# A key-maximum pass over pairs of context chunks: relu of a score difference on ScalarE, add and maximum on VectorE, four PSUM bank pairs in turn, and context loads issued from GpSimd's queue

## What is computed

```python
q = (query @ Wq + bq).reshape(B, Nq, H, D)            # H = 16 heads, D = 16
k = (key_value @ Wk + bk).reshape(B, Nkv, H, D)       # Nkv = 12544
attn = clip(einsum('bhqd,bhkd->bhqk', q, k) * scale, -10000, 10000)
attn = softmax(attn, axis=-1)
x = einsum('bhqk,bhkd->bqhd', attn, v).reshape(B, Nq, Cq) @ Wo + bo
```

## Time and profile before

| | before |
|---|---|
| median of three runs | 1149.45 us |
| the profiled execution's own time | 1144.78 us |
| its span, first to last instruction | 1142.9 us |
| TensorE matmul busy over the span | 944.5 us (83%) |
| VectorE busy | 645.1 us (56%) |
| ScalarE busy | 537.1 us (47%) |
| GpSimd busy | 173.4 us (15%) |
| mean granted TensorE clock | 0.927 |

### The profile page before, as it was taken

One profiled execution on the slowest core, in us unless ns is written; L12 is line 12 of the kernel. 1 busy time (PEld: TensorE's weight loads), 2 busy tenths in 40 slices (PEclk: granted clock), 3 DMA queues, 4 the chain that ended last, 5 costly groups with the idle time before them and its releaser, 6 DMA issues.

```text
span 1142.9 us, 21211 instructions
## 1 busy us (share of the span) xinstructions
PE 944.5 (83%) x7651; PEld 699.5 (61%) x7651; DVE 645.1 (56%) x936; ACT 537.1 (47%) x626; POOL 173.4 (15%) x93
## 2 busy tenths in 40 slices
PE   3878888758999999999988758885999989999414
PEld 2545555536777777777756546554887868887303
DVE  5778999872111122222252144994878767778592
ACT  2787888627666666666645512100333323333011
POOL 4000000131111111111175022133003030000000
PEclk9988999779999999999998769998999999999765
DMA  7213121154565665555634332112001000000000
GB/s 211 74 42 122 48 71 57 32 129 87 130 140 130 144 145 128 128 128 128 143 82 98 112 102 56 29 50 55 1 1 38 1 6 1 1 1 1 1 0 5
DMA packets 37319, 81.73 MB, mean 72 GB/s; under 512 B 9553, under 2 KB 17426, under 8 KB 37138
## 3 DMA queue, kind: packets, MB, share of 16 engines
q1 hardware_dynamic: 37266, 81.01, 28.5%
HBM read 41.54 MB, written 0.13 MB: 36 GB/s over the span
## 4 chain that ended last, share of the span: by engine, by line
PE 44%; issue 20%; DVE 11%; SPq 9%; ACT 8%; DMA 6%; POOL 1%; DVEq 1%; ACTq 0%; POOLq 0%
PE ps L1498 9%; SPq L310 8%; DMA ks<-khl 6%; PE ps L1291 5%; PE ps L1508 5%; PE ps L1519 4%; PE ps L1303 4%; PE ps L1245 4%; PE ps L1273 4%; PE ps L1500 2%; DVE cm L813 1%; ACT pr L555 1%; ACT oacc L555 1%; PE ps L1282 1%; ACT khl L592 1%
## 5 line engine op out<-in xcount | busy, mean ns | idle before, releaser
L617 ACT ACTIVATE pr<-ps 128x1024 f32<-128x1024 f32 x196 | 199.9, 1026 | 131.6 <-DVEq L966 128.2
L1291 PE MATMUL ps<-qs,ks 128*128 128x256 f32 x784 | 146.4, 309 | 23.2 <-DMA ks<-khl 14.6
L1245 PE MATMUL ps<-ks 128*128 128x448 f32 x448 | 135.2, 424 | 32.3 <-ACT pr L555 13.5
L1291 PEld LDWEIGHTS ps<-qs,ks 128*128 128x128 f32 x784 | 106.0, 190 | 66.3 <-issue 38.1
L1498 PE MATMUL ps<-ks,ct 128*128 128x512 f32 x448 | 126.1, 404 | 6.9 <-issue 4.2
L813 DVE TENSOR_REDUCE cm<-ps 128x1 f32<-128x896 f32 x112 | 120.7, 1085 | 16.1 <-PE ps L1245 14.7
L1245 PEld LDWEIGHTS ps<-ks 128*128 128x128 f32 x448 | 80.8, 206 | 75.4 <-DVE cm L813 25.1
L1303 PE MATMUL ps<-pr,v 128*17 128x128 f32 x3136 | 125.3, 278 | 0.2 <-ACT pr L617 0.2
L847 DVE SCALAR_TENSOR_TENSOR khl<-ps,bk,khl 128x448 fp32r<-128x448 f32 x56 | 38.2, 683 | 151.5 <-ACT khl L592 151.5
L695 ACT ACTIVATE pr<-ps 128x1024 f32<-128x1024 f32 x56 | 57.6, 1029 | 110.5 <-DVE ps L1096 109.7
L405 POOL TENSOR_TENSOR ct<-raw,ct 128x896 fp32r<-128x896 f32 x14 | 30.6, 2188 | 498.5 <-ACT ct L537 498.5
(11 more groups left out here) (260 smaller groups left out, 1307.4 us busy)
## 6 DMA issues: line engine op xcount, KB each, us to landing
ks<-khl SPq DMA_DIRECT2D x168, 224.0 KB, 4.8
raw<-in_ctxT SPq DMA_DIRECT2D x36, 448.0 KB, 3.8
raw<-in_ctxT SPq DMA_DIRECT2D x54, 224.0 KB, 4.3
ffw<-in_mask_q SPq DMA_DIRECT2D x1, 1568.0 KB, 9.3
ffw<-in_W1T SPq DMA_DIRECT2D x1, 1024.0 KB, 4.9
ffw<-in_W2T SPq DMA_DIRECT2D x1, 1024.0 KB, 7.3
pr<-in_Wq SPq DMA_DIRECT2D x1, 1024.0 KB, 5.0
pr<-in_Wkt SPq DMA_DIRECT2D x1, 1024.0 KB, 7.3
```

What stands on the lines that cost most here:

```text
L617: nc.scalar.activation(pr[:, (HALVES * b + u) % 4, :], bank(2 * (u % 2), 2), ACT.Exp).then_inc(S["e0_exp"], 1)
L1245: last = mm(ps[:, bank + n, 0:NB], qn[:, h, :], kn[:, b, t, n * NB:(n + 1) * NB], start=True, stop=True)
L1291: last = mm(ps[:, 2 * z + k // 2, (k % 2) * 256:(k % 2) * 256 + 256], ks_v[:, b, gg, t * P:(t + 1) * P], qs[:, gg * 256:gg * 256 + 256], s ...
```

## The change

- The pass goes over seven pairs of chunks. With b the scores of the first chunk of a pair and a those of the second, it takes max(a, b) as b + relu(a - b). TensorE computes a - b directly, from keys of the difference: ScalarE makes the first chunk's keys (`base_keys`), VectorE the second's minus the first's (`key_differences`, a scalar_tensor_tensor of 128x896 that replaces ScalarE's activation). ScalarE writes relu(a - b) of every head as fp32 into one of four `stage` slots (`above_base`), and VectorE adds b from PSUM and takes the maximum over the columns with the custom instruction of the second layer (`head_max`).
- Every head now needs both tiles. TensorE's order in a pair is `FULL`: for each head a unit "above" and a unit "base", and after heads 2, 5, 8 and 11 a unit that projects the next pair, two blocks of four matmuls in all. Units take the four bank pairs strictly in turn, and each unit waits until the unit four places earlier has been read (`slot_free`). The last pair has `LAST`, with the sum pass's first keys and values as such units.
- The context comes by two transfers a chunk from GpSimd's queue directly into `ct`; the loads by SP into `raw` and ScalarE's copies go away, and so does the fill of `acc`, with `acc` itself and its folding at the end.
- The mask's seven sums become seven maxima on VectorE in the first pair (`any_kept`, 128x448 each). The weight sums move behind the fifth pair.
- Keys have a second buffer in the first part of `ks`; GpSimd fills the ones there only once the sixth pair is done.

```diff
-HEAD_BANKS = (0, 2, 6)
-def head_bank(b, h):
-    return HEAD_BANKS[(h + b) % 3]
...
+UNITS = 2 * H
+SLOTS = 4
+def pair_order(extra):
+    order = []
+    for h in range(H):
+        order += [("above", h), ("base", h)] + extra.get(h, [])
+    return order
+FULL = pair_order({2: [("keys", 0)], 5: [("keys", 1)], 8: [("diff", 0)], 11: [("diff", 1)]})
+LAST = pair_order({1: [("key0", 0)], 4: [("key0", 1)], 7: [("value0", 0)], 9: [("value0", 1)],
+                   11: [("value0", 2)], 13: [("value0", 3)]})
+def unit_bank(order, kind, i):
+    return 2 * (order.index((kind, i)) % 4)
...
-        kn = ks[:, k0_at + HQ:].rearrange("p (b t n) -> p b t n", b=2, t=2)
+        kn = [ks[:, k0_at + HQ:].rearrange("p (e t n) -> p e t n", e=2, t=2),
+              ks[:, 0:4 * CH].rearrange("p (e t n) -> p e t n", e=2, t=2)]
...
-        acc = pr_flat[:, 0:4 * CH].bitcast(BF16).rearrange("p (j n) -> p j n", j=8)
-        stage = [oacc_flat[:, 0:CH // 2].bitcast(BF16),
-                 pr_flat[:, 4 * CH:4 * CH + CH // 2].bitcast(BF16)]
+        stage = pr_flat[:, 0:SLOTS * CH].rearrange("p (i k n) -> p i k n", i=SLOTS, k=2)
...
-            nc.gpsimd.memset(acc, -3.0e38).then_inc(S["acc_init"], 1)
+            def load_max0(c):
+                if c >= 2:
+                    pool.wait_ge(S["m0_proj"], 2 * c + 2)
+                pool.dma_start(ct[:, c % 2, X_AH, :], ctx_t[0:P, c * CH:(c + 1) * CH]).then_inc(S[f"m0_ct{c % 2}"], 16)
+                pool.dma_start(ct[0:64, c % 2, X_B, :], ctx_t[P:CKV, c * CH:(c + 1) * CH]).then_inc(S[f"m0_ct{c % 2}"], 16)
+            load_max0(0)
+            load_max0(1)
...
-            nc.gpsimd.memset(ks[96:P, 0:k0_at - 8 * T].bitcast(F32), 1.0).then_inc(S["ks_ones"], 1)
+            nc.gpsimd.memset(ks[96:P, 4 * CH:k0_at - 8 * T].bitcast(F32), 1.0).then_inc(S["ks_ones"], 1)
...
+            for c in range(2, NCH):
+                load_max0(c)
             split_lo0(0, 0)
+            pool.wait_ge(S["e0_lo"], 2)
+            pool.wait_ge(S["m0_head"], UNITS * NSUP)
+            nc.gpsimd.memset(ks[96:P, 0:4 * CH].bitcast(F32), 1.0).then_inc(S["ks_ones"], 1)
+            pool.wait_ge(S["ks_ones"], 2)
...
-            def split_max0(c, b):
-                act.wait_ge(S["m0_raw"], 32 * (c + 1))
-                act.wait_ge(S["m0_proj"], 4 * c + 4)
-                nc.scalar.copy(ct[:, b, X_AH, :], raw[:, 0, :])
-                nc.scalar.copy(ct[0:64, b, X_B, :], raw[0:64, 1, :]).then_inc(S["m0_split"], 1)
-            def key_block_max0(c, b, i):
-                t, n = i // 2, i % 2
-                if i == 0:
-                    act.wait_ge(S["m0_head"], H * c + H)
-                act.wait_ge(S["m0_proj"], 4 * c + i + 9)
-                nc.scalar.activation(kn[:, b, t, n * NB:(n + 1) * NB], ps[:, 4 + i % 2, 0:NB], ACT.Identity,
-                                     bias=bk0[:, t:t + 1]).then_inc(S["m0_keys"], 1)
...
+            def base_keys(s, t):
+                if t == 0:
+                    act.wait_ge(S["m0_head"], UNITS * s)
+                act.wait_ge(S["m0_proj"], 4 * s + t + 5)
+                at = unit_bank(FULL, "keys", t) if s > 0 else 4 + 2 * t
+                nc.scalar.activation(kn[s % 2][:, 0, t, :].rearrange("p (k n) -> p k n", k=2), ps[:, at:at + 2, 0:NB],
+                                     ACT.Identity, bias=bk0[:, t:t + 1]).then_inc(S["m0_keys"], 1)
...
+            def above_base(s, h):
+                at = unit_bank(FULL if s < NSUP - 1 else LAST, "above", h)
+                act.wait_ge(S["m0_head"], UNITS * s + 2 * h + 1 + UNITS)
+                act.wait_ge(S["m0_red"], H * s + h - SLOTS + 1 + H)
+                nc.scalar.activation(stage[:, h % SLOTS], ps[:, at:at + 2, 0:NB], ACT.Relu
+                                     ).then_inc(S["m0_staged"], 1)
+            for t in range(2):
+                base_keys(0, t)
+            for s in range(NSUP - 1):
+                for h in range(H):
+                    above_base(s, h)
+                    if h in (3, 6):
+                        base_keys(s + 1, (3, 6).index(h))
+                    if h == 8 and s == NSUP - 2:
+                        act.wait_ge(S["m0_proj"], 4 * (NSUP - 1) + 6)
+                        split_hi0(0, 0)
+                if s == 4:
+                    act.wait_ge(S["ld_ffw"], 32)
+                    for k in range(2):
+                        nc.scalar.activation(scrap, ffw[:, 2048 * k:2048 * k + 2048], ACT.Abs,
+                                             accum_out=wsum[:, k:k + 1]).then_inc(S["wsum"], 1)
+                        act.wait_ge(S["wsum"], k + 1)
...
+            def key_differences(s, t, buf, at):
+                dve.wait_ge(S["m0_head"], UNITS * s)
+                dve.wait_ge(S["m0_keys"], 2 * s + t + 1)
+                dve.wait_ge(S["m0_proj"], 4 * s + t + 7)
+                V.scalar_tensor_tensor(kn[buf][:, 1, t, :].rearrange("p (k n) -> p k n", k=2), ps[:, at:at + 2, 0:NB],
+                                       bk0[:, t:t + 1],
+                                       kn[buf][:, 0, t, :].rearrange("p (k n) -> p k n", k=2).bitcast(F32),
+                                       ALU.add, ALU.subtract).then_inc(S["m0_diff"], 1)
+            def head_max(s, h, order=FULL):
+                at = unit_bank(order, "base", h)
+                dve.wait_ge(S["m0_head"], UNITS * s + 2 * h + 2 + UNITS)
+                dve.wait_ge(S["m0_staged"], H * s + h + 1 + H)
+                V.memset(pause2[:, h % 2:h % 2 + 1], 0.0)
+                nc.vector.tensor_tensor_reduce(
+                    out=stage[:, h % SLOTS], in0=ps[:, at:at + 2, 0:NB], in1=stage[:, h % SLOTS],
+                    scale=1.0, scalar=-3.0e38, op0=ALU.add, op1=ALU.max,
+                    accum_out=cm[:, h:h + 1]).then_inc(S["m0_red"], 1)
+            def merge_max0(s):
+                dve.wait_ge(S["m0_red"], H * s + 2 * H)
+                V.tensor_tensor(mx[:, :], mx[:, :], cm[:, :], ALU.max).then_inc(S["m0_merge"], 1)
+            def any_kept(s):
+                if s == 0:
+                    dve.wait_ge(S["ld_mask"], 16)
+                V.tensor_reduce(cnt[:, s:s + 1], mflat4[:, CH // 2 * s:CH // 2 * (s + 1)], AX_X, ALU.max
+                                ).then_inc(S["mask_any"], 1)
+            def pair_max0(s, buf, masks=False):
+                dve.wait_ge(S["m0_merge"], s + 1)
+                for h in range(H):
+                    head_max(s, h)
+                    if h in (9, 12):
+                        t = (9, 12).index(h)
+                        key_differences(s + 1, t, 1 - buf, unit_bank(FULL, "diff", t))
+                    if masks and 4 <= h < 4 + NSUP:
+                        any_kept(h - 4)
+                merge_max0(s)
...
-            n = CH // 2
-            while n >= CH // 8:
-                link(V.tensor_tensor(acc[:, :, 0:n], acc[:, :, 0:n], acc[:, :, n:2 * n], ALU.max))
-                n //= 2
-            link(V.tensor_reduce(mx_e[:, :, 1], acc[:, :, 0:CH // 8], AX_X, ALU.max))
...
+            def slot_free(order, s, q):
+                if s is None or q >= 4:
+                    kind, i = order[q - 4]
+                    back = 0
+                else:
+                    kind, i = FULL[len(FULL) + q - 4]
+                    back = -1
+                if kind == "above":
+                    pe.wait_ge(S["m0_staged"], H * (s + back) + i + 1 + H)
+                elif kind == "base":
+                    pe.wait_ge(S["m0_red"], H * (s + back) + i + 1 + H)
+                elif kind == "keys":
+                    pe.wait_ge(S["m0_keys"], 2 * (s + 1 + back) + i + 1)
+                elif kind == "diff":
+                    pe.wait_ge(S["m0_diff"], 2 * (s + 1 + back) + i + 1 + 2)
+                elif kind == "key0":
+                    pe.wait_ge(S["e0_klo"], 2 * i + 2 + 2)
+                elif kind == "value0":
+                    pe.wait_ge(S["e0_v"], min(2 * i + 2, TPC) + 1)
+            def project_max0(s, e, t, at):
+                if t == 0:
...
+            def head_scores(s, buf, kind, h, at):
+                t = h // 8
+                if h % 8 == 0 and kind == "above":
+                    pe.wait_ge(S["m0_keys"], 2 * s + t + 1)
+                    pe.wait_ge(S["m0_diff"], 2 * s + t + 3)
+                for n in range(2):
+                    last = mm(ps[:, at + n, 0:NB], qn[:, h, :],
+                              kn[buf][:, 1 if kind == "above" else 0, t, n * NB:(n + 1) * NB],
+                              start=True, stop=True)
+                last.then_inc(S["m0_head"], 1)
...
+            def pair_max0(s, buf, first=False):
+                for q, (kind, i) in enumerate(FULL):
+                    if first and q < 4:
+                        if q >= 2:
+                            pe.wait_ge(S["m0_diff"], q - 2 + 1 + 2)
+                    else:
+                        slot_free(FULL, s, q)
+                    at = unit_bank(FULL, kind, i)
+                    if kind in ("above", "base"):
```

(74 more changed lines are left out.)

197 lines of the change are left out of this document (39 added, 158 removed).

## The result

The changed kernel takes 1169.58 us (median of four runs, 1168.49 to 1171.68) against 1150.09 us before; the ratio is 1.0172, with a 95% interval of 1.0153 to 1.0191. It is 19.5 us slower. The forecast was 1165.0, within 1139 to 1186.

A forecast was written before the change was run, and what follows sets the result against it. VectorE was taken to set the pace of the maximum pass now. With the clock granted the change gave -8.4 us, clock falls +24, so +15.6 on the 1149.45 us median: 1165.0 us, range 1139 to 1186.

The forecast's parts named there:

- The ring: Six full pairs: TensorE, ScalarE and VectorE wait for each other in turn; 28.3 us a pair, 3.1 more than now.
- The clock: TensorE's idle times in the maximum pass: 16 falls of the granted clock at 1.5 us each, 24 us (0 to 48).
- The rival that the clock stays granted: Maximum pass: TensorE's idle times pass without a clock fall, giving 1141.0 us; chance 0.18.
- Weight sums: Behind the fifth pair: two sums of 2.04 us hold ScalarE, at most 0.4 covered, 3.7 us; plus one clock fall.
- Start: Before the first head: early root gain spent on 16 matmuls, 28.4 against 28.09 us; first custom instruction 1.7 later.
- Last pair: Seventh pair, with the sum pass's key and value units: 36 us, plus three clock falls.
- End: Last merge to TensorE's start: small VectorE instructions beside GpSimd's, between 1.2 and 7.4 us, taken as 4.2 instead of 9.6.
- The other rivals: Maximum pass: cheap clock falls, 1149 us, chance 0.07; VectorE sets the pace, 1075, 0.03; GpSimd-queue loads late, 1207, 0.05.

The follow-up runs named there:

- the kernel with fillers: The changed kernel with eight unread matmuls ahead of the base units of heads 10 and 13 in the six full pairs: 1161.15 us.
- the best kernel: Changed kernel with key differences, last-pair reads and key blocks one head earlier, first context loads behind the root, GpSimd's remainder moved, weight sums spread: 1104.64 us.

## Why the prediction was right, and where not

The direction, the place and the cause were right: the ring made a pair longer than two chunks, through the wait of head 10's base unit for the key difference. Along the steps of the forecast, in us, with the profiled execution:

| step | forecast | measured |
|---|---|---|
| first custom instruction (28.4 + 1.7) | 30.1 | 35.24 |
| six pairs: 169.8, and 12 falls of 1.5 | 187.8 | 6 x 30.6 = 183.8 |
| weight sums, 3.7, and one fall | 5.2 | 37.80 - 30.6 = 7.2 |
| last pair, 36, and three falls | 40.5 | 42.2 |
| end | 4.2 | 4.5 |
| TensorE's start | 267.8 | 272.95 |

At TensorE's start the forecast is 5 us early, as much as at the first custom instruction: the terms behind the start were off by -4.0, +2.0, +1.7 and +0.3, which cancel. So it is in part luck that the forecast of 15.6 us slower came within 4 us of the measured 19.5.

- *The ring*, 28.3 us a pair. At full clock it takes 29.25. In the kernel with fillers the relus of heads 6, 9, 12 and the next head 3 start at 132.83, 138.23, 144.93 and 156.66: steps of 5.40, 6.70 and 11.73 against 5.22, 6.52 and 11.37. Each is short by 0.2 to 0.4. A projection unit lies 1.48 in TensorE's queue (first matmul at 36.91, next unit at 38.39) where the single blocks gave 2 x 0.70, which is 0.08 of it; the rest is spread over links that no single row sets apart. The price of 1.15 for the key difference, chosen between 1.08 and 1.37, is what the trace shows.
- *The clock*. The term had the right cause: without the waits, by fillers or by order, the full pairs have no fall but the one of the weight sums. The price of a fall, 1.5 us, was near the measured 1.4. The count was wrong: one fall a pair instead of two, so 1.4 us a pair instead of 3.0, while the last pair had four instead of three. The rule of the Trainium skill that the forecast weighed (TensorE: Matmul & The Clock Gate, "A second HAM failure mode: psum-queue depth-cycling") let the 24 us stand, 18 of them in the six pairs; there the falls cost 8.4. The trace agrees with it in that each fall of these pairs came with an idle time of TensorE of 2.4 us and more. The cycling alone does not do it: with the difference one head earlier the same four bank pairs are cycled, and the stretch of 85.36 to 110.60 is at 1.00. The rival that the clock stays granted was not met.
- *The ring and the clock together* came within 4 us only since 0.9 too little and 1.6 too much a pair cancel in part.
- *Weight sums*, 5.2 against 7.2: behind them the clock was at 0.50 from 193 to 203 us, where the forecast had put in one short fall.
- *Start*. This step failed. It took the root to be the only thing ahead of the first projection and gave 28.4 for the first head; the weights' loads stood beside it, had no term in the sum, and let the casts start 5.5 us later than before because of the very loads that the change moved forward. The loads behind the root give the forecast's picture: first projection at 17.07, where it had 17.7, and first custom instruction at 30.05, where it had 30.1.
- *Last pair*. 42.2 against 40.5; with its reads one head earlier 27.06, so 15 of these 42 us were the order, with the falls that came with it. The forecast described the chain, and didn't ask what the same units would take in another order; nor did it for the full pairs.
- *End*. 4.2 had been taken between 1.2 and 7.4. The stretched instructions end with GpSimd's: the merge from 268.44 to 270.02 beside L395 from 267.92 to 269.99, the negation from 270.27 to 272.20 beside L398 from 270.07 to 272.16. That is the rule of the Trainium skill, SBUF — State Buffer, "Who interferes with whom", and the trace agrees; the bound of 7.4 was too high because L395 and L398 take 4.2 us here, not the 6.1 of the earlier trace rows, and L395 began 0.5 us before the merge.
- *The other rivals*: the loads of GpSimd's queue landed in 4.2 and 4.5 us at the median, and in the middle pairs no projection waited for one. VectorE did not set the pace, and doesn't in the best kernel either (19.3 of 24.8 us).

Behind the wrong count of falls stands a reading: the forecast took from the kernel before that each of five idle times was followed by a low clock within 0.4 us. That doesn't hold for the third:

```profile
79.72 1.06 PE L1245 MATMUL ps<-ks 128*128 128x448 f32 x4 [2.89 <-ACT oacc L555]
```

Its four matmuls run at full speed, and the clock falls at 81.3, 1.6 us later. A further fall, at 95.0, has no wait above 0.85 us in the 10 us ahead of it. So the count of waits was no count of falls.

What stays open: why in the changed kernel the fall follows the wait before head 10 and not the one before head 13, where with the loads behind the root it followed both in the first pair and neither in the second; and how far the old form could be brought by its own start and end, which no run shows.

## What to carry to other kernels

In a ring of buffers, give each reader its place in its engine's order by the moment its input is ready, not one item later: moving the readers by one head was worth 32 us in the full pairs and 15 in the last one, together more than twice what the whole change cost. Before adding up busy time for a new form, follow one round of the ring through all queues; and when work is moved forward at the start, list every load that is under way beside it. Side work belongs where its engine waits anyway: in the pair form a weight sum there cost less than 0.1 us, while in the old form the weight sums, merely set apart, won nothing.

## What the runs showed of the hardware

- Two idle times of TensorE of nearly the same length, 2.40 and 2.38 us, 8 us apart in a pair of the changed kernel: behind the first the clock fell to 0.50, behind the second it stayed at 1.00. With the context loads behind the root both were passed at 1.00 in the second pair. In the kernel before, four of five idle times of 2.3 us and more were followed by a fall within 0.3 us and one after 1.6 us.
- With eight matmuls that nobody reads in each idle time of 2.4 us the clock was 1.00 from 35 to 186 us, where the weight sums come, and a pair was 1.4 us shorter.
- Four context loads from GpSimd's queue, issued from 1.54 us on, made the weights' loads on SP's queue, issued at 2.53 and 2.98 us with and without them, land 8.6 and 9.0 us after their issue instead of 3.5 and 3.3, and the casts behind them start 6.3 us later (13.66 against 7.40).
- VectorE's layer norm step of 128x256 takes 0.41 us with no GpSimd fill beside it, 3.68 beside a GpSimd fill of 3.51 and 6.73 beside one of 6.49.
